# Slot sums over the last four tiles in every step, the last tile's turns and division moved behind the first experts, one transpose of the attention maxima, first rows placed on chip

## The reference, cut to what matters

```python
patches, n_list = patchify(x, P1, P2)                      # 32 x 36 rows of 768
h = concatenate([einsum('bnk,ok->bno', patches, W) + b, txt], axis=1)   # 32 x 113 rows of 256
h = h + attn(layernorm(h))                                 # 16 heads of 16, rope, softmax over 113 keys
logits = einsum('tzd,ed->tze', xln, phi_w) + phi_b         # xln = layernorm(h): 3616 rows x 2048 slots
D = softmax(logits, axis=3)                                # over the 32 slots of an expert
C = softmax(logits, axis=2)                                # over the 64 experts
X_tilde = einsum('tznp,tzd->npd', D, x)                    # sums over ALL rows
X_tilde = tanh(layernorm(X_tilde))
Y_tilde = einsum('npd,ndH->npH', X_tilde, expert_w) + expert_b
h = h + einsum('tznp,npH->tzH', C, Y_tilde)
```

## Time and profile before

| | |
|---|---|
| median of 3 runs | 952.89 us (952.81 to 953.38) |
| the profiled execution | 952.25 us |
| its span in the trace | 950.6 us |
| PE busy | 905.8 us, 95% |
| PE weight load / DVE / POOL / ACT busy | 755.3 / 711.5 / 527.8 / 503.0 us |

### The profile page before, as it was taken

One profiled execution on the slowest core, in us unless ns is written; L12 is line 12 of the kernel. 1 busy time (PEld: TensorE's weight loads), 2 busy tenths in 40 slices (PEclk: granted clock), 3 DMA queues, 4 the chain that ended last, 5 costly groups with the idle time before them and its releaser, 6 DMA issues. The chain is left out here.

```text
span 950.6 us, 21865 instructions
## 1 busy us (share of the span) xinstructions
PE 905.8 (95%) x7764; PEld 755.3 (79%) x7764; DVE 711.5 (75%) x1065; ACT 503.0 (53%) x817; POOL 527.8 (56%) x490
## 2 busy tenths in 40 slices
PE   6999999999998968999999999999999989999997
PEld 4877888888887646788888888888887748888886
DVE  1466777777776799999999999999998755555552
ACT  1156555555555365766676676676664353333331
POOL 1257233322232287899999999999998351000100
PEclk9999999999999978999999999999999999999999
DMA  7501111111111153323323223223228995777660
GB/s 251 192 26 43 44 43 43 41 41 43 40 54 30 42 118 79 84 71 96 81 69 99 77 72 99 72 79 100 67 72 309 360 390 193 236 242 239 225 191 18
DMA packets 99973, 111.01 MB, mean 117 GB/s; under 512 B 12228, under 2 KB 91204, under 8 KB 93908
## 3 DMA queue, kind: packets, MB, share of 16 engines
q1 hardware_dynamic: 97760, 106.23, 36.3%
q0 software_dynamic: 1376, 3.70, 1.0%
q10 hardware_dynamic: 788, 0.44, 0.2%
HBM read 72.14 MB, written 38.21 MB: 116 GB/s over the span
## 5 line engine op out<-in xcount | busy, mean ns | idle before, releaser
L1409 PE MATMUL slots_p_sum<-slots_x,slots_disp 128*128 128x256 f32 (+1 forms) x928 | 206.7, 380 | 2.7 <-DVE sums_bias L1039 2.2
L1409 PEld LDWEIGHTS slots_p_sum<-slots_x,slots_disp 128*128 128x128 f32 (+1 forms) x928 | 173.7, 190 | 27.2 <-issue 4.2
L1151 POOL TENSOR_TENSOR slots_comb<-slots_comb,slots_cmax 128x1024 f32<-128x1024 f32 x56 | 108.1, 1949 | 11.3 <-DVE slots_cmax L944 9.9
L1553 PE MATMUL slots_p_turn<-slots_y_parts,slots_hi 128*128 128x512 f32 (+1 forms) x464 | 111.0, 391 | 0.0
L1162 POOL TENSOR_TENSOR slots_comb<-slots_comb,slots_csum 128x2048 f32<-128x2048 f32 x28 | 101.4, 3621 | 7.4 <-DVE slots_csum L921 7.4
L427 POOL TENSOR_TENSOR attend_stack<-attend_rope_a,attend_rope_b 113x128 f32<-113x128 f32 x128 | 54.4, 457 | 90.7 <-DVE attend_rope_b L383 90.7
L1156 POOL TENSOR_TENSOR slots_disp<-slots_disp,slots_dsum 128x2048 f32<-128x2048 f32 x27 | 98.4, 3646 | 0.0
L1553 PEld LDWEIGHTS slots_p_turn<-slots_y_parts,slots_hi 128*128 128x128 f32 (+1 forms) x464 | 84.1, 186 | 18.0 <-issue 0.4
L1197 POOL DMA_DIRECT2D out<-slots_o x29 | 15.9, 548 | 144.1 <-DVE slots_o L1078 144.1
L1442 PE MATMUL slots_logits<-phi_hi,slots_xt_hi 128*128 128x512 f32 x224 | 78.8, 434 | 7.6 <-ACT slots_comb L1261 5.3
L931 DVE TENSOR_TENSOR slots_disp<-slots_logits,slots_dmax 128x512 f32<-128x512 f32 x112 | 77.5, 692 | 4.2 <-PE slots_p_sum L1409 0.3
(11 more groups left out here) (156 smaller groups left out, 1854.9 us busy)
## 6 DMA issues: line engine op xcount, KB each, us to landing
combine_t<-slots_ct SPq DMA_DIRECT2D x224, 128.0 KB, 2.4
slots_comb<-combine_t SPq DMA_DIRECT2D x14, 1024.0 KB, 5.5
slots_ct<-combine_t SPq DMA_DIRECT2D x14, 1024.0 KB, 5.8
expert_w<-wexp SPq DMA_DIRECT2D x8, 1024.0 KB, 9.3
slots_disp<-wexp SPq DMA_DIRECT2D x8, 1024.0 KB, 14.0
h<-attend_h_out SPq DMA_DIRECT2D x32, 113.0 KB
slots_h_t<-h SPq DMA_DIRECT2D x28, 128.0 KB, 2.3
slots_x<-h SPq DMA_DIRECT2D x28, 128.0 KB, 2.1
```

Of the source, the lines that this page charges most:

```text
L1151: nc.gpsimd.tensor_tensor(m, m, cmax[0:rows, shalf(i)].unsqueeze(2).broadcast_to([rows, SLOTS // 2, EXPERTS]), ALU.subtract).then_inc(csub ...
L1409: last = nc.tensor.matmul(p_sum[u % 2][:, i, :], disp[d][part].rearrange("p n s -> p (n s)")[:, 128 * block:128 * block + 128], x[d][part] ...
L1553: return nc.tensor.matmul(p_o[c % 2][0:rows], hi[c % 2][:, e, 0:rows], y_parts[:, e].rearrange("p i c -> p (i c)"), start=e == 0, stop=e = ...
```

## The change

1. **First rows.** DVE writes the 36 patch rows of image 0 straight from PSUM into `h_in[0]` and then tile 0 into `emb_sb`; ACT's DMA copies the rows of image 1 from `emb_sb` to `h_in[1]`, ahead of the write to `emb`. No load waits for `emb` there. ACT's split of the weights stands behind its first attention step; the ninth tile is embedded ahead of step -1 and not of step 0.
2. **Maxima.** DVE writes the maxima into a tensor `maxima` of their own, laid out so that one transpose puts them at the right partitions. DVE adds them to `qt` to make `qmax`; ACT's copy goes. The stack has four columns where it had one, of which each head group has one set to 1, so the final scores multiply 20 rows of a block and not 17.
3. **Slot sums.** A step t sums its two units over the last four tiles, max(t-4, 0) to t-1, in place of a fixed group. Each unit's sums are still over four tiles; steps 2 to 4 have 2, 3 and 4 tiles in place of one. After the loop units 0 and 1 lack four tiles, 2 and 3 three, 4 and 5 two, 6 and 7 one.
4. **Tail.** DVE takes the last tile's sum over `comb` behind the first unit (not ahead of it), and divides `comb` itself behind the third, where POOL did. PE turns `comb` behind the second and the fourth expert block; SP stores it and loads the first tiles of the combination in between the last expert blocks. The weight ring has 11 places: three new ones, loaded in steps 2 to 4, three in `disp`, loaded in the last three steps, the four own places and one more in `disp`. So 5 blocks and not 8 wait for a place.

```diff
-    turn = {-4: range(0, 1), -3: range(1, 3), -2: range(3, 6), -1: range(6, 8), 0: range(8, tiles)}
+    turn = {-4: range(0, 1), -3: range(1, 3), -2: range(3, 6), -1: range(6, tiles), 0: range(0)}
...
             dve.wait_ge(mm_done, t + 1)
+            if t == 0:
+                first_rows(acc[0], bias)
...
+    maxima = sb("maxima", [T, GH, 32])
...
-                nc.vector.tensor_reduce(stack[par][:, 0, :, DH].rearrange("p (g j) -> p j g", j=GH),
+                nc.vector.tensor_reduce(maxima[:, :, DH:DH + GROUPS],
...
+            if scores:
+                dve.wait_ge(qmax_ps_ok, val(b + 1))
+                dve.wait_ge(q_ok, val(b + 1))
+                wait_for(dve, shifted_ok, b)
+                nc.vector.tensor_tensor(qmax[:], qt[par][:], p_q[:, 0, 0:T].unsqueeze(1).broadcast_to([128, GROUPS, T]),
+                                        ALU.add).then_inc(qmax_ok, 1)
...
+        def first_rows(acc, bias):
+            nc.vector.tensor_tensor(h_in[0][0:PATCHES, :], acc[0:PATCHES, 0:C], bias[0:PATCHES], ALU.add).then_inc(h_ld[0], 16)
...
-            if scores:
-                act.wait_ge(qmax_ps_ok, val(b + 1))
-                wait_for(act, shifted_ok, b)
-                nc.scalar.activation(qmax[:], p_q[:, :, 0:T], ACT.Copy).then_inc(qmax_ok, 1)
...
+        act.wait_ge(emb_ready, 1)
+        act.dma_start(h_in[1][0:PATCHES, :], emb_sb[PATCHES:2 * PATCHES, 0]).then_inc(h_ld[1], 16)
         e_scalar(act, -4)
-        act.wait_ge(emb_out[0], 16)
-        for b in range(2):
-            act.dma_start(h_in[b][0:PATCHES, :], emb[b * PATCHES:(b + 1) * PATCHES, :]).then_inc(h_ld[b], 16)
...
-                turn_stack(p_q, par, 0, qmax_ps_ok)
+                nc.tensor.transpose(p_q[:, 0, 0:T], maxima[:], ident[0:T, 0:T]).then_inc(qmax_ps_ok, 1)
...
+    w = spare + in_disp[0:3] + w_slots + in_disp[3:4]
...
+            if static(t) and LAST - 2 <= t:
+                sp.wait_ge(sum_ok, PER * (t - 1))
+                load_expert(SPARE + t - LAST + 2)
...
+            if static(t) and 1 < t <= 1 + SPARE:
+                load_expert(t - 2)
...
         load_weights(0, 0, 128)
-        store(LAST, LAST % 2)
-        load_weights(1, 1, 128)
         for i in range(WRING, EB):
             load_expert(i)
+            if i == WRING:
+                store(LAST, LAST % 2)
+                load_weights(1, 1, 128)
...
         for u in range(UNITS):
             gather(u)
             if u >= 1:
                 scale(u - 1)
             if u == 0:
+                combine_sum(LAST, LAST, 128)
                 dve.wait_ge(eb_in, 16 * EPB)
+            if u == 2:
+                normalise_combine(LAST, LAST % 2)
...
-                group = (c - 1) // TG
-                tiles = [(0, SHORT)] if c <= TG else [(d % RING, 128) for d in range(TG * group - TG + 1, TG * group + 1)]
-                done = t - (c - 1) % TG
-                if u == 0 and c > TG:
-                    pe.wait_ge(disp_ok, val(done - 1))
-                pe.wait_ge(kept_ok, val(done))
+                tiles = [(d % RING, 128 if d else SHORT) for d in range(max(c - TG, 0), c)]
+                if not static(t) or t > 1:
+                    pe.wait_ge(disp_ok, val(t - 1))
+                pe.wait_ge(kept_ok, val(t))
...
-            add_products(u, last_group, TILES + (u >= UNITS // 2)).then_inc(sum_ok, 1)
+            left = [(t % RING, 128) for t in range(LAST - TG + 1 + u // PER, LAST + 1)]
+            add_products(u, left, TILES + (u >= UNITS // 2)).then_inc(sum_ok, 1)
...
         products(3)
-        turn_weights(LAST, LAST, 2)
-        turn_weights(LAST, LAST, 3)
         turn(0)
         turn(1)
         for i in range(EB):
...
                 turn(i + 2)
+            if i in (1, 3):
+                turn_weights(LAST, LAST, i - 1)
+                turn_weights(LAST, LAST, i)
```

More of the change, by code:

```diff
@@ L510, in step @@
                 nc.scalar.activation(piece(phi_hi, i), piece(phi_raw, i), ACT.Copy).then_inc(phi_hi_ok, 1)
+        act.wait_ge(emb_ready, 1)
+        act.dma_start(h_in[1][0:PATCHES, :], emb_sb[PATCHES:2 * PATCHES, 0]).then_inc(h_ld[1], 16)
         e_scalar(act, -4)
-        act.wait_ge(emb_out[0], 16)
-        for b in range(2):
-            act.dma_start(h_in[b][0:PATCHES, :], emb[b * PATCHES:(b + 1) * PATCHES, :]).then_inc(h_ld[b], 16)
-        steps(act, step, e_scalar, follow, BATCH)
+        steps(act, step, lambda act, b: b == -2 and e_scalar(act, -3), follow, BATCH)
         rest(lambda: keep_values(BATCH), lambda: high(BATCH, False))
@@ L698, in slots @@
     p_sum = [pb(f"p_sum{i}", [128, 2, C]) for i in range(2)]
-    w = w_slots + [disp[i][:].rearrange("p n s -> p (n s)").rearrange("p (j k c) -> p j k c", j=EPB, k=KC)
-                   for i in (5, 6, 7, 0)]
+    in_disp = [disp[i][:].rearrange("p n s -> p (n s)").rearrange("p (j k c) -> p j k c", j=EPB, k=KC) for i in (5, 6, 7, 0)]
+    spare = [sb(f"spare_w{i}", [128, EPB, KC, C])[:] for i in range(SPARE)]
+    w = spare + in_disp[0:3] + w_slots + in_disp[3:4]
     WRING = len(w)
@@ L1159, in step @@
                     add_sum(*units[1])
-                pool.wait_ge(crec_ok, val(t + 1))
-                m = comb[c % 2][0:rows]
-                nc.gpsimd.tensor_tensor(m, m, csum[0:rows, 1].unsqueeze(2).broadcast_to([rows, SLOTS, EXPERTS]),
-                                        ALU.mult).then_inc(comb_ok, 1)
+                if not last:
+                    pool.wait_ge(crec_ok, val(t + 1))
+                    m = comb[c % 2][0:rows]
+                    nc.gpsimd.tensor_tensor(m, m, csum[0:rows, 1].unsqueeze(2).broadcast_to([rows, SLOTS, EXPERTS]),
+                                            ALU.mult).then_inc(comb_ok, 1)
         def follow(pool, b):
@@ L1523, in apply @@
             last.then_inc(y_ps_ok, 1)
-        last_group = [(t % RING, 128) for t in range(LAST - TG + 1, LAST + 1)]
         products(0)
```

51 lines of the change are left out of this document (28 added, 23 removed).

## The result

The changed kernel takes 957.12 us (median of 5, 954.48 to 957.78) against 952.87 us (median of 5, 951.95 to 953.38): the ratio is 1.004, with a 95% interval of 1.0025 to 1.0056. It is slower by about 4 us, where 951.7 was forecast. (Measured once more beside the kernel before, in experiment 9, it took 956.32 against 954.01, with an interval of 0.9999 to 1.0045: there the two can't be told apart.) The profiled execution took 957.78, its span is 956.1.

A forecast was written before the change was run, and what follows sets the result against it. PE was taken to bound the routing, a dependency loop through xn the attention, and the last weights the tail. Terms -8.1 + 1.3 + 8.3 - 2.7 = -1.2 gave a forecast of 951.7 us, range 946.5 to 956.

The forecast's parts named there:

- Start, -8.1: Before the attention loop: PE's 6.84 us wait for xn goes, plus about 1.3 of clock; bounds -6.8 and -8.7.
- the 1.3 for the clock: At the start, 36 records behind PE's wait ran slowed; without the wait about 1.3 us should not be lost.
- Attention loop, +1.3: 26 full attention steps: DVE's added work delays xn, each step about 0.05 us longer; bounds -1 and +4.
- the slack: Attention step: room between xn being written and PE turning it, taken as 0.05 to 0.1 us.
- the rival with a chance of 0.04: Attention loop hangs on PE alone: 26 steps save up to 0.3 us each, time 942.6; chance 0.04.
- Early steps, +8.3: Routing steps 2 to 4: added sums 10.4 us, less 0.5 hidden and 1.6 of clock; bounds 5.5 and 9.9.
- 6 tiles times 8 records: Routing steps 2 to 4: 48 added records at about 0.216 us each, 10.4 us in all.
- the 2.1 that I took off: Early routing steps: 0.5 us hidden under ACT's copies and 1.6 returned by the clock, subtracted from 10.4.
- Steady steps, 0: Later routing steps: PE reaches the newest tile's disp 0.66 us after POOL finishes it, so no cost.
- Tail, -2.7: After the routing loop: the last block, waiting for weights, starts at 779.4, not 782.12; bounds 0 and -9.7.
- the 9.6 that I gave the computation: Tail: computation alone could end about 9.6 us earlier, 6.1 before the first turn and 3.5 over four units.
- The rival that I held against the forecast: Attention loop: DVE's add paces it, 26 steps cost 4 to 5.2 us, time 954.4 to 955.6; chance 0.15.

The follow-up runs named there:

- experiment 9: The changed kernel measured once more, unaltered, beside the kernel before: 956.32 us, ratio 1.0022.
- experiment 1: The kernel before with only the first rows placed on chip: 944.59 us against 952.4, ratio 0.991.
- Experiments 7 and 10: One program, run twice: the changed kernel with the store behind the weight blocks and the old slot sums; 937.98 and 939.97 us, both ratio 0.9852 to the kernel before.
- Experiment 3: The changed kernel with the first half of each unit summed newest tile first in steps 2 to 4: 955.58 us, ratio 1.0028 to the kernel before.
- experiment 4: The changed kernel with SP's store and the combination's loads behind the last five weight blocks: 945.69 us against 952.4 before, ratio 0.9927.
- experiment 6: The kernel before with only the slot sums over the last four tiles: 966.26 us against 952.7, ratio 1.014.

## Why the prediction was wrong, point by point

What failed most are two prices: that of the early sums, by 3.9 us, and that of the tail, by 3.5. The change-over, for which no term stood, adds 2.1.

- **Start, -8.1.** Right in mechanism: 7.8 us in the time of experiment 1, and the 1.3 for the clock belong in it, since PE's first records ran at full clock. The exact figure is partly luck: at the first maximum 9.1 were gained, more than the bound of 8.7, and 1.0 of it went again in the second step, where the clock fell. In four of the seven traces with both parts that step took 7.8.
- **Attention loop, +1.3.** Wrong in sign; measured -1.5. For the short kind of step the delays along DVE were forecast to 0.02 us, and so was `xn`, 0.12 later. The step that failed is the slack: I took 0.05 to 0.1 "(0.2 less the time from a semaphore to its waiter)". In the changed trace PE loads `xn` 0.08 after its end, so of the 0.20 all of 0.12 could be spent. And the long kind of step was left out: there DVE's wait took in the whole add, and the step is 0.06 to 0.1 shorter. That the saving showed at all was the rival with a chance of 0.04, at a fifth of its 7.8 us.
- **Change-over.** No term stood for it; it cost 2.1. The clock fell in the last attention step. Experiments 7 and 10 show that one program can have this fall and not have it; why it is frequent with the new start (six of seven) and absent with the old one (none of four) stays open.
- **Early steps, +8.3.** Measured +12.2. The product of records and price held (1.73 for each added tile and step). What failed is the step "6 tiles times 8 records", at 0.216 each: it took a group of mixed tiles at the price of one with full tiles. The mixing adds 1.36 us in each of three steps, 4.1 in all. Experiment 3 took half of it off PE by the order alone. The rest, 10.4 + 4.1 - 12.2 = 2.3 hidden or returned by the clock, is near the 2.1 that I took off. The clock gave back 0.9 and not 1.6: from the start of a step's logits to the start of its sums it took 7.21 us in step 3 (349.98 to 357.19) where it took 8.25 (354.87 to 363.12), 7.30 in step 4 where it took 7.32 (370.35 to 377.67), and 7.53 in step 2 where it took 7.37. The other 1.35 were hidden in the waits behind the sums, where 0.5 was forecast. The waits of 2.12 us ahead of the logits stayed, and a stretch at half clock stayed behind each. By the rule of the page "TensorE: Matmul & The Clock Gate" of the Trainium skill, section "HAM oscillation — how this bites in real kernels", nothing would have come back; the trace agrees in step 4 and not in step 3.
- **Steady steps, 0.** Right to 0.01 us in 23 steps: no wait for the newest `disp`.
- **Tail, -2.7.** Tail and combination together are +0.8, which is 3.5 off. The first turn of a unit came at 741.93, 13.95 after the last maximum over `comb`, where it was 20.08 before: the 6.1 are right. The mechanism behind it, the last blocks wait for SP's queue, is right, and experiment 4 shows it: with the weights in time the tail is 9.95 shorter than before, near the 9.6 that I gave the computation. The sizes are off: the store was issued at 758.77, which is 754.1 on the scale of before, as I counted (754.3). The last block's matmuls began at 785.51, or 780.8 on that scale, against 779.4: from the store to that block it took 26.7 and not 25.1 (six loads of 2.5 are 15.0 and not the 14.8 of my sum, which is a small part of it). What I left out is the clock: behind the waits of 3.88 and 3.08 PE was at half speed, so the last block took 0.87 longer and the combination 1.2. The later start, 1.4, with these 0.9 and 1.2 is the 3.5. I also took the queue for the limit that can't be moved; it was the order of its list.
- **The port lock.** The new division on DVE did hold POOL up, as the Trainium skill's page "SBUF — State Buffer" has it in its section "SBUF: two separate sides", and the trace agrees on the blocking:

```profile
743.57 2.93 POOL L1210 TENSOR_TENSOR slots_e_rstd<-slots_e_mv,slots_e_power 128x2 f32<-128x2 f32 x1
743.65 2.28 DVE L1085 TENSOR_TENSOR slots_comb<-slots_comb,slots_csum 128x2048 f32<-128x2048 f32 x1
```

POOL's power takes 0.73 in its other turns and 2.93 here, and ends 0.57 after the division. By the records it began 0.08 ahead of the division; which of the two held the lock first they don't show. No run isolates what this costs.

Summed: the forecast's -1.2, and against it the attention loop -2.8, the change-over +2.1, the early steps +3.9, tail and combination +3.5 make +5.5, the measured difference of the spans. The rival that I held against the forecast, the add on DVE pacing the loop, was not what made it slower.

## What to carry to other kernels

An engine that issues DMAs goes through its list in order, as SP did here (12.9 us in front of one store): before a store that waits for late work put any load whose place is already free, or the load's consumer pays; look for a stretch in which the DMA engines are half idle and a transfer is late behind it. Moving matmuls from a tail that hangs on something else into a stretch where the engine is full can lose their whole time (experiment 6); with the hold-up gone the tail still gave back 5.6 of 10.4 us (experiment 7). And when a group of matmuls is priced from another, take the price from one with the same mixture of row counts.

## What was not expected of the hardware

- Matmuls over 32 rows, alternating with such over 128 rows (same columns), cost 0.19 us more for each change, in either direction: pairs follow at 0.62 us where 0.43 is the price without one, fours at 1.05 where it is 0.86, and 16 records take 5.08 in one order and 4.39 in the other. Whether it is the row count or the place of the 32 rows among the partitions was not separated.
- Two executions of one program, on two chips, differ by 1.2 us in one attention step (7.83 and 9.03) at the place where PE's work thins out, the second with the granted clock at 0.50 there.
